# Where GpSimd clears the value tile and sets the second buffer's spare rows in a one-core decoder layer

## The reference

```python
x = x + attn(layernorm(x))          # 16 heads of 8, keys and values through a latent of 32
x = x + xattn(layernorm(x), ctx, mask)   # 1024 queries on 6404 context rows, width 128
x = x + ffn(layernorm(x))           # gate/up/down, 352 wide, inputs and weights quantized in blocks of 16

# attn:
scores = einsum(qh, k_rec) / sqrt(d)
scores = scores * exp(-0.01 * abs(t_q - t_k))
out = softmax(scores) @ v_rec @ W_o
```

## Time and profile before

| | us |
|---|---|
| median of 3 runs (lowest, highest) | 560.83 (559.85, 562.63) |
| the profiled execution | 562.73 |
| its span, first to last instruction | 560.6 |
| PE / DVE / ACT / POOL busy in it | 502.9 / 368.1 / 334.6 / 168.5 |

### The profile page before, as it was taken

One profiled execution on the slowest core, in us unless ns is written; L12 is line 12 of the kernel. 1 busy time (PEld: TensorE's weight loads), 2 busy tenths in 40 slices (PEclk: granted clock), 3 DMA queues, 4 the chain that ended last, 5 costly groups with the idle time before them and its releaser, 6 DMA issues.

```text
span 560.6 us, 9755 instructions
## 1 busy us (share of the span) xinstructions
PE 502.9 (90%) x3494; PEld 329.3 (59%) x3494; DVE 368.1 (66%) x874; ACT 334.6 (60%) x659; POOL 168.5 (30%) x283
## 2 busy tenths in 40 slices
PE   6539899999999999999779979979798997989997
PEld 5305433333333333323558969979797897878896
DVE  7789988887887788701664465647666466664354
ACT  3454877777878787889254826537274472637420
POOL 7800023544444444333433221321213122210000
PEclk9857999999999999999989989989899898999999
DMA  8797300043006100054564424333233433400000
GB/s 241 227 271 152 68 20 3 4 98 75 1 3 143 30 1 4 1 147 129 177 208 125 147 64 133 93 113 91 77 113 89 115 90 89 137 16 1 5 6 6
DMA packets 21811, 49.21 MB, mean 88 GB/s; under 512 B 3948, under 2 KB 9268, under 8 KB 21188
## 3 DMA queue, kind: packets, MB, share of 16 engines
q1 hardware_dynamic: 21012, 47.87, 30.5%
q0 software_dynamic: 224, 0.54, 0.4%
q10 hardware_dynamic: 528, 0.18, 0.1%
HBM read 43.67 MB, written 4.72 MB: 86 GB/s over the span
## 4 chain that ended last, share of the span: by engine, by line
PE 68%; DVE 22%; issue 4%; ACT 3%; DMA 1%; POOL 1%; DVEq 0%; ACTq 0%; POOLq 0%
PE banks L923 47%; PE banks L1032 11%; PE banks L1177 6%; DVE banks L749 6%; DVE logits L830 2%; PE banks L1043 2%; DVE fa L866 1%; ACT probs L614 1%; PE banks L928 1%; DMA mring<-in_mask_BxSxS_ik 1%; DVE xn L714 1%; DVE qc_lo L796 1%; DVE fa L865 1%; DVE fa L861 1%; DVE f_small L857 1%
## 5 line engine op out<-in xcount | busy, mean ns | idle before, releaser
L614 ACT ACTIVATE probs<-banks 128x512 f32<-128x512 f32 x288 | 158.9, 600 | 40.6 <-PE banks L923 34.8
L749 DVE CUSTOM_DVE_ANT_0 banks<-banks,decay 128x1024 f32<-128x1024 f32 x128 | 155.0, 1243 | 30.1 <-PE banks L923 29.4
L923 PE MATMUL banks<-operands 112*128 112x512 bf16 (+4 forms) x736 | 147.5, 332 | 21.4 <-DMA operands<-query_parts 13.1
L923 PEld LDWEIGHTS banks<-operands 115*128 115x128 bf16 (+1 forms) x736 | 55.2, 98 | 127.1 <-ACT probs L614 57.5
L923 PEld LDWEIGHTS banks<-mem,pT 128*128 128x128 f32 (+1 forms) x816 | 109.6, 197 | 7.9
L923 PE MATMUL banks<-mem,pT 128*128 128x128 f32 (+1 forms) x816 | 113.2, 282 | 0.0
L830 DVE CUSTOM_DVE_ANT_0 logits<-banks,mring 128x512 f32<-128x512 f32 (+1 forms) x102 | 67.5, 668 | 49.6 <-PE banks L923 26.6
L635 ACT ACTIVATE pT<-banks 128x512 f32<-128x512 f32 (+1 forms) x104 | 60.4, 581 | 52.4 <-PE banks L1177 52.4
L489 POOL TENSOR_SCALAR mring<-mring 128x1024 f32<-128x1024 int32 (+1 forms) x55 | 52.4, 953 | 87.9 <-DMA mring<-in_mask_BxSxS_ik 85.5
L470 POOL TENSOR_SCALAR_AFFINE_SELECT probs<-probs 128x128 f32<-128x128 f32 x128 | 37.1, 293 | 115.7 <-ACT probs L614 114.1
L1032 PE MATMUL banks<-probs,v_ext 128*32 128x512 f32 x512 | 68.2, 604 | 0.7 <-ACT probs L614 0.5
(11 more groups left out here) (168 smaller groups left out, 500.7 us busy)
## 6 DMA issues: line engine op xcount, KB each, us to landing
mring<-in_mask_BxSxS_ik SPq DMA_DIRECT2D x47, 512.0 KB, 3.6
operands<-key_parts SPq DMA_DIRECT2D x24, 192.0 KB
operands<-query_parts SPq DMA_DIRECT2D x21, 192.0 KB
key_parts<-operand_parts SPq DMA_DIRECT2D x10, 256.0 KB, 3.6
query_parts<-operand_parts SPq DMA_DIRECT2D x4, 384.0 KB, 3.7
mring<-in_mask_BxSxS_ik SPq DMA_DIRECT2D x8, 130.0 KB, 2.2
operands<-shift_parts SPq DMA_DIRECT2D x48, 4.0 KB, 1.8
operands<-query_parts SPq DMA_DIRECT2D x6, 96.0 KB
```

Source lines behind the costliest of these rows:

```text
L614: act.activation(probs[:, to, :], PS[:, u % 3, :], ACT.Exp).then_inc(s_p, 1)
L749: dve.tensor_tensor_reduce(out=rows, in0=rows, in1=decay[:, off:off + S], scale=1.0, scalar=-3.0e38, op0=ALU.mult, op1=ALU.max, accum_out= ...
L923: return pe.matmul(o, a, b, start=start, stop=stop, skip_group_check=alone)
```

## The change

On GpSimd the clear of `v_ext` and its ones move from behind `rstd` to behind the index table, and the memsets of the second buffer's spare rows get a wait for VectorE's clamp of that table.

```diff
             pool.wait_ge(s_rstd, 1)
+            pool.wait_ge(s_xn, NH)
+            pool.iota(iota_d[:, :], pattern=[[-1, 2 * S - P]], base=S - P, channel_multiplier=1).then_inc(s_iota, 1)
+            pool.wait_ge(s_iota, 2)
             link(pool.memset(v_ext[:, :, :, :], 0.0))
             pool.memset(v_ext[:, :, :, HD:HD + 1], 1.0).then_inc(s_vclear, 1)
             pool.wait_ge(s_vclear, 1)
-            pool.wait_ge(s_xn, NH)
-            pool.iota(iota_d[:, :], pattern=[[-1, 2 * S - P]], base=S - P, channel_multiplier=1).then_inc(s_iota, 1)
-            pool.wait_ge(s_iota, 2)
             link(pool.memset(wg_raw[FF - NKW * P:P, :, :].rearrange("p (a n) d -> p a n d", a=2)[:, :, NKW, :], 0.0))
...
+            pool.wait_ge(s_iota2, 1)
             for w, value in ((KL, ONES_PAIR), (QL, 0.0), (QU, 0.0), (KU, ONES_PAIR)):
                 pool.memset(spare_rows(1, w), value).then_inc(s_spare[1], 1)
             pool.wait_ge(s_spare[1], 4)
```

## The result

The changed kernel takes 557.19 us (median of 6 runs, 555.75 to 558.25) against 560.85 (6 runs): ratio 0.9928, 95% interval 0.9905 to 0.9951, a gain of 3.7 us where 4.9 were forecast. A second measurement of the same two kernels gave 557.68 (12 runs) against 560.73 (24 runs): ratio 0.995, interval 0.9931 to 0.9969, a gain of 3.1. The profiled execution took 557.16 us with a span of 555.1. In the changed kernel lines behind the edit are one higher (L715 for L714, L726 for L725, L733 for L732, L750 for L749).

The account below looks back on a forecast made before the run. The start was taken as a serial stretch ending at the first row maximum, which bounds what follows. 2.86 + 1.4 + 1.0 - 0.4 = 4.9 us, from the median 560.83 to 555.9; range 554.5 to 558.3.

Parts of the forecast that it names:

- the two stalls: VectorE's `xn` instructions and its clamp stood still until GpSimd's memsets ended: 3.1 us and 1.8 us.
- the order of the waits: GpSimd's spare-row memsets wait for the clamp until 22.8, end at 29.8, ahead of SyncE's first look at 37.
- the clock falls anyway: Rival: TensorE's clock still falls at the start; 2.86 and 1.0 of the clamp remain, 3.9 us, 557.0; chance 0.20.
- Term 1, `xn`: Start of the kernel: without the 3.1 us stall of VectorE's eight `xn`, the first key product comes 2.86 us sooner.
- Term 2, the clock: Key products: TensorE's idle stretch shrinks, its clock stays full, and L725's second half gains a further 1.4 us.
- Term 3, the clamp: VectorE's clamp of the table loses its 1.8 us stall; 0.8 is covered by the loads, 1.0 gained.
- Term 4, transfers: Stores and loads ahead of the first row-maximum products queue behind the context load: 0.4 us lost, bounds 0 and 0.9.
- the transfers are the bound: Rival: loads hold the first products until 34.0 instead of 35.72, a gain of 1.7, 559.1; chance 0.08.
- Their sum: Gain at the first row maximum: 2.86 + 1.4 + 1.0 - 0.4 = 4.9 us.
- What the start gains should reach the end: After the first row maximum no wait looks at a time of day; that stretch stays 522.8 us, within 1 us.
- the clear of `v_ext` would hold L725: Rival: the moved clear stalls VectorE's scaling like `xn`; second L725 near 17.9, 1.8 us left, 559.0; chance 0.04.
- the slower rival: Row-maximum pass: TensorE's clock rises later, 8 further low steps cost 1.0 each, ending 3 us slower, 564; chance 0.02.

Follow-up runs that it names:

- e2: Kernel before with only the wait for the clamp added, the clear of v_ext left in place: 560.73 us, ratio 0.9993.
- e1: Changed kernel without the wait for the clamp, so only the clear of v_ext moved: 563.40 us, ratio to the kernel before 1.0038.
- e3: Kernel before with 20 more throw-away transposes ahead of those of xn, filling TensorE's idle stretch: 559.42 us, ratio 0.9968.
- e5: Changed kernel with the five feed-forward weight loads started behind the spare-row memsets: 556.97 us, ratio to the kernel before 0.9938.
- e8: Changed kernel without the wait, the five feed-forward DMA starts between the second and third spare-row memset: 559.57 us, ratio to the kernel before 0.9986.
- e4: Changed kernel without the three groups of four throw-away transposes between the small weight products: 556.61 us, ratio to the kernel before 0.9916.
- e4_again: Changed kernel without the throw-away transposes between the small weight products, measured a second time: 557.97 us, ratio to the kernel before 0.9934.
- b_again: Kernel before, unchanged, run for a second profile: 561.08 us, ratio 1.0011.
- e7: Changed kernel without the wait, the four spare-row memsets ahead of the five feed-forward DMA starts: 560.42 us, ratio to the kernel before 0.9994.
- b_third: Kernel before, unchanged, run for a third profile: 560.88 us in one run.
- e6: Changed kernel with feed-forward loads started behind the memsets and the clamp done by GpSimd instead of VectorE: 561.18 us, ratio to before 1.0005.

## Why the prediction was right, and where its size was off

The direction, the two stalls and the order of the waits were as written. The measured 557.19 lies in the range, in its upper part: 3.7 us gained for 4.9 (3.1 in the second measurement). By the time alone the rival "the clock falls anyway" (557.0) fits better than the forecast (555.9); the traces decide against it, and where the missing gain went the last two points take up. Term by term, from the three profiles of the kernel before and two of the changed one (and e2's, whose start is the old one up to the clamp):

- *Term 1, `xn`: right, and shown by e1.* With the clear alone moved, the eight `xn` take 2.14 us too. Forecast 2.86 for the first key product. It started at 15.41, 15.84, 15.75 and 15.85 (e2) and then at 12.58 and 12.94: 2.95. The three later starts among the old ones have a clock that fell before it; where it fell only behind (15.41) the difference to 12.58 is 2.83.
- *Term 2, the clock: right, and shown by e3.* Forecast 1.4 beyond term 1. The second scaling of KL started at 18.69, 18.46, 19.02, 19.60 and then at 14.58, 14.93: 4.19 in all, 1.24 beyond term 1. In e3, which has the old stall of `xn` and the full clock, it started at 17.43, and 2.85 of the way to 14.58 is term 1. The rival that the clock falls anyway did not come up in either profile of the changed kernel, nor in those of e1 and e5 to e8, where 1.00 was granted from 11 to 16 us. It does come up without the throw-away transposes (e4).
- *Term 3, the clamp: mis-sized.* The step "its stall is 27.84 - 26.05 = 1.8 us" took one execution for all (and even there it is 1.65, since the clamp alone takes 1.15 and not 1.0). The durations 2.80, 1.30 and 2.48 over 1.15 make 1.0 on average. Alone (e2) it is worth nothing measurable. By the traces that is because the old order of the clear happened to bring VectorE to the clamp at the last memset. With the clear moved, leaving out the wait costs 6 us (e1). The two edits do not add: apart they give +2.1 and -0.5 us, together -3.1 to -3.7. I had priced the wait by the stall of the kernel before and never by the stall that term 1 would create without it.
- *Term 4, transfers: right in kind.* Forecast 0.4 late, first products near 31.8; they came at 31.06 and 31.73. The rival that the transfers are the bound (34.0, 559.1) is refuted by these starts. But the term varies: between the issue of the first-query loads and the first product lay 6.0 and 6.3 us there, 8.1 in e4_again and 10.8 in e8. A range of 0 to 0.9 was too narrow for it.
- *Their sum* at the first row maximum, forecast 4.9: starts 37.82, 36.35, 37.83 against 32.23, 32.90, on average 4.8. Right, but with luck: the stall was taken 0.8 too long, and the wait for the loads behind it, forecast at 0.8 + 0.4 = 1.2, was nothing and 0.40. The two errors cancel.
- *"What the start gains should reach the end": not all of it did.* The rest lasted 522.8, 522.3 and 521.0 before and 522.9 and 522.4 after, 0.6 more; the spans differ by 4.1 on average. The part that varies is cross-attention (286.1 to 287.8 in the unchanged kernel). The last 0.4 to 1.0 between 4.1 and the medians' 3.7 and 3.1 is within what five profiles can't tell. How unsure the way from the start to the end is, e4 shows: its start is 2 to 4 us later than the changed kernel's, and its time the same.

The rival that the clear of `v_ext` would hold L725 is refuted (1.47 us for two beside it), and the slower rival too: the clock in the row-maximum pass rose behind two slow steps with a context transpose (at 41.66 and 43.37, before at 47.24 and 48.95), not later.

## What to carry to other kernels

A long memset on GpSimd is not free background work: look at which one-input instructions of VectorE from SBUF to SBUF lie beside it (here two kinds of `tensor_scalar`), and put it beside two-input or PSUM work instead, which was not held here. When an edit makes an engine arrive earlier, price what it will now meet, not only what it met before; here that was four memsets instead of the last one. And where a stall hangs on which of two engines comes first by tenths of a microsecond, one profile gives one side of it: take two or three profiles of the unchanged kernel before sizing such a term.

## What the runs showed of the hardware that was not expected

- An idle stretch of TensorE of 2.5 us was followed by a fall from the 2.4 to the 1.2 GHz level in four of four profiles, but the fall came at about 13.4 (e2), 13.7 (b_again), 15.1 (b_third) or 15.8 us (first profile), and L725's second start lay anywhere in 1.1 us. Filled with throw-away transposes, no fall (e3, one profile). Without the stretch of 2.5 us but with patchy work instead, the clock fell too, at about 9.6 and 9.4 (e4).
- A clamp of VectorE that waits for a row of memsets does not reliably get in between two. In b_again and e3 it asked 1.52 and 0.50 us behind the start of the third and ran ahead of the fourth; in e7 it asked 0.40 us behind the third's start and waited for both; in e1 it waited for four. What decides is open.
- VectorE's clamp lengthens a DMA start of GpSimd from 0.80 to 1.68 us and is not lengthened by it (e8); the start ended 0.13 us behind the clamp. In e7 a start ran beside the clamp's last 0.7 us, took 0.83 and ended 0.12 behind it.
- A subtraction of VectorE held by GpSimd's reading clamp ended at 18.70, while that clamp ran to 20.43 by the trace (e6), so it did not wait for its end. Spans on GpSimd are rough, and this was seen once.
